# Three gathers of expert rows in flight instead of two

## The reference

```
x = x + attention(layernorm(x))
h = layernorm(x)                                  # 4096 tokens of 128
logits = h @ router_w.T                           # 16 experts
score  = sigmoid(top-1 logit), 0 for the others
routed = sum over experts of down(up * silu(gate)), gate and up from (h * score) @ gate_up_proj[expert]
shared = (silu(h @ shared_gate_w.T) * (h @ shared_up_w.T)) @ shared_down_w.T     # 512 wide
x = x + shared + routed
```

## Time and profile before

| | |
|---|---|
| Median of 3 runs | 231.84 us (228.6 to 233.66) |
| Profiled execution, its own time | 231.57 us |
| Its span, first to last instruction | 229.8 us |
| TensorE, VectorE, ScalarE, GpSimd busy | 88%, 72%, 52%, 53% of the span |
| Mean granted clock of TensorE | 0.946 of full speed |
| The 32 gathers on GpSimd | 32.5 us busy, 33.8 us idle ahead of them |

### The profile page before, as it was taken

The page is one execution under the profiler, slowest core; times in us unless marked ns, Lnnn a source line. Parts: engine busy times, 40 slices in busy tenths (PEclk is TensorE's granted clock), DMA queues, the critical chain, the costliest instruction groups (busy, mean ns, idle before and its releaser), DMA issues.

```text
span 229.8 us, 3715 instructions
## 1 busy us (share of the span) xinstructions
PE 202.2 (88%) x1081; PEld 158.4 (69%) x1081; DVE 165.8 (72%) x437; ACT 119.6 (52%) x237; POOL 122.2 (53%) x143
## 2 busy tenths in 40 slices
PE   7874998889899887689885999999998999999972
PEld 7533754657667866578563889999886877778641
DVE  1599999999999955546677377976435667676773
ACT  2423565566584686732555367554444555636441
POOL 5003336749966866446747666731006675666540
PEclk9998899999999997755999799999999999999999
DMA  4999994120010111111124547533341131322514
GB/s 118 270 333 337 297 228 130 61 93 26 13 35 28 35 47 47 35 51 35 35 59 106 115 106 184 137 84 94 91 130 34 34 91 44 85 79 58 140 34 137
DMA packets 33399, 23.54 MB, mean 102 GB/s; under 512 B 2914, under 2 KB 30564, under 8 KB 33380
## 3 DMA queue, kind: packets, MB, share of 16 engines
q1 hardware_dynamic: 30752, 18.85, 30.9%
q0 software_dynamic: 2048, 4.26, 6.6%
q10 hardware_dynamic: 580, 0.20, 0.4%
HBM read 13.87 MB, written 9.44 MB: 101 GB/s over the span
## 4 chain that ended last, share of the span: by engine, by line
PE 48%; DVE 34%; issue 6%; ACT 3%; DMA 3%; SPq 2%; POOL 1%; ACTq 1%; DVEq 0%
PE quad_banks L1217 8%; DVE qkv L784 7%; PE quad_banks L1218 7%; PE quad_banks L1219 7%; PE bank L1373 4%; DVE ss L802 4%; DVE st L748 4%; PE bank L1276 3%; DVE s_spl L881 3%; DVE rn L810 3%; PE bank L1278 2%; PE bank L1277 2%; DMA w_qkv<-L_attn_Wv 2%; PE bank L1337 2%; DVE ss L806 2%
## 5 line engine op out<-in xcount | busy, mean ns | idle before, releaser
L457 POOL DMA_INDIRECT h_rows<-y_slots,gpos x32 | 32.5, 1015 | 33.8 <-DMA y_slots<-yg 16.7
L390 POOL DMA_INDIRECT x_slots<-h_rows,pos x32 | 31.1, 972 | 16.0 <-issue 8.8
L876 DVE TENSOR_TENSOR s_act<-quad_banks,sg_act 128x512 f32<-128x512 f32 x32 | 22.0, 689 | 20.7 <-ACT sg_act L550 16.2
L550 ACT ACTIVATE sg_act<-quad_banks 128x512 f32<-128x512 f32 x32 | 19.2, 600 | 32.0 <-PE quad_banks L1219 25.3
L362 POOL TENSOR_TENSOR qkv<-qkv,rn 128x512 f32<-128x512 f32 x16 | 16.9, 1078 | 32.5 <-DVE rn L810 32.5
L881 DVE TENSOR_TENSOR s_spl<-s_act,s_spl 128x512 fp32r<-128x512 f32 x32 | 25.7, 809 | 1.7 <-issue 1.7
L1168 PE MATMUL quad_banks<-w_c,xT 128*128 128x384 f32 x64 | 23.5, 492 | 2.2 <-DVE qkv L784 1.4
L556 ACT CAST s_spl<-s_act 128x512 fp32r<-128x512 f32 x32 | 19.6, 614 | 5.6 <-PE bank L1278 4.5
L784 DVE SCALAR_TENSOR_TENSOR qkv<-quad_banks,rs,b_qkv 128x384 f32<-128x384 f32 x32 | 17.8, 602 | 1.8 <-PE quad_banks L1168 1.7
L1276 PE MATMUL bank<-s_spl,sdT 128*128 128x512 f32 x32 | 14.6, 456 | 4.5 <-DVE s_spl L881 4.0
L1168 PEld LDWEIGHTS quad_banks<-w_c,xT 128*128 128x128 f32 x64 | 11.2, 194 | 9.5 <-issue 5.0
(11 more groups left out here) (167 smaller groups left out, 529.4 us busy)
## 6 DMA issues: line engine op xcount, KB each, us to landing
h_rows<-x_slots SPq DMA_DIRECT2D x47, 66.0 KB, 1.9
y_slots<-yg SPq DMA_DIRECT2D x11, 256.0 KB, 2.4
xT<-L_attn_x_turned SPq DMA_DIRECT2D x8, 256.0 KB, 6.5
xres<-L_attn_x SPq DMA_DIRECT2D x8, 256.0 KB, 6.2
w_raw<-L_ffn_gate_up_proj SPq DMA_DIRECT2D x4, 512.0 KB, 5.1
out<-xres SPq DMA_DIRECT2D x8, 256.0 KB
x_slots<-zero_rows SPq DMA_DIRECT2D x1, 1056.0 KB, 14.1
x_slots<-zero_rows SPq DMA_DIRECT2D x1, 990.0 KB, 10.6
```

Of the source, the lines that this page charges most:

```text
L390: g.indirect_dma_start(out=x_slots, out_offset=bass.IndirectOffsetOnAxis(ap=pos[:, t:t + 1], axis=0), in_=h_rows[:, t, :], in_offset=None) ...
L457: g.indirect_dma_start(out=h_rows[:, t, 0:D], out_offset=None, in_=y_slots, in_offset=bass.IndirectOffsetOnAxis(ap=gpos[:, t:t + 1], axis= ...
L876: v.tensor_tensor(s_act[:, k % 2], pair[:, 2 * (k % 2) + 1], sg_act[:, k % 2], ALU.mult).then_inc(s_act_rdy, 1)
```

## The change

The number of gathers in flight becomes a constant, IN_FLIGHT = 3. There are three semaphores instead of two, gather t counts on semaphore t mod 3, and before it is issued GpSimd waits for gather t-3 in place of t-2. In `gathered(c)` VectorE waits on all three, each with the count of those of the first 4(c+1) gathers that fall to it.

```diff
+    IN_FLIGHT = 3
...
-        gath = [sem("gath0"), sem("gath1")]
+        gath = [sem(f"gath{r}") for r in range(IN_FLIGHT)]
...
             for t in range(NT):
-                if t >= 2:
-                    pool.wait_ge(gath[t % 2], 16 * (t // 2))
+                if t >= IN_FLIGHT:
+                    pool.wait_ge(gath[t % IN_FLIGHT], 16 * (t // IN_FLIGHT))
                 g.indirect_dma_start(out=h_rows[:, t, 0:D], out_offset=None, in_=y_slots,
                                      in_offset=bass.IndirectOffsetOnAxis(ap=gpos[:, t:t + 1], axis=0)
-                                     ).then_inc(gath[t % 2], 16)
+                                     ).then_inc(gath[t % IN_FLIGHT], 16)
...
             def gathered(c):
-                for landed in gath:
-                    dve.wait_ge(landed, 16 * (c + 1) * Q // 2)
+                for r, landed in enumerate(gath):
+                    dve.wait_ge(landed, 16 * len(range(r, Q * (c + 1), IN_FLIGHT)))
                 return h_rows[:, Q * c:Q * c + Q, 0:D]
```

## The result

| | before | after |
|---|---|---|
| Median of 4 runs each | 232.75 us (228.6 to 234.28) | 261.2 us (259.35 to 266.34) |
| Profiled execution | 231.57 us | 259.35 us |
| Its span, mean granted clock | 229.8 us, 0.946 | 257.6 us, 0.901 |

The changed kernel was slower: ratio 1.132, 95% interval 1.108 to 1.156. (The ratio is of the fast executions alone, those within 1.5% of the fastest of their kernel, so it is a little above the 1.122 of the two medians.) The forecast was 231.6 us. A second timing of the unaltered changed kernel gave 265.07 us, and a single run at a third time gave 231.72 us. Both numbers belong to the result, and most of what follows is about the difference between them.

What follows compares the result with a forecast made beforehand. The prediction took TensorE's shared-expert work to bound the end, with no gather on the chain. Span 229.8 us, minus 0 plus 0 (up to +0.2), and 1.77 us around it gave 231.6 us; range 228.6 to 233.6 us.

Steps and rivals of the forecast that it cites:

- The waits on GpSimd: GpSimd's gathers: ordinary waits for landings vanish, 31 steps take 40.8 us, GpSimd ends 6 to 10 us sooner; worth 0.
- Who could use the earlier landing: VectorE's sums and the output stores: they stand behind shared-expert products at TensorE's pace, so they don't move: 0.
- three signs of being wrong: End moves over a microsecond with TensorE's last chunk in place; gathers' mean well above 1.02 us; sums with gathered rows idle.
- The cover: Shared expert on TensorE hides the gathers; if it were gone, up to 7.7 us would show.
- The waits on VectorE: VectorE's sums with gathered rows: eight added semaphore waits, 0 to 0.2 us on the path, taken as 0.
- the transfers: DMA queues: gathers form a denser stream, over by about 217, and the last three stores have the queues to themselves: 0.
- The rule weighed: VectorE operations with two SBUF inputs contend with GpSimd reading SBUF; three gathers ran longer, 1.28 to 1.46 us.
- the slow rival: Gathers slowed beside VectorE's splits and sums: 237.0 us, deciding from a step of 1.60 us; chance 0.04.
- Gathers that bind in ordinary executions: Rival: slow landings use up the end's cushion of about 1.1 us, so the change gives 228.6 us; chance 0.13.
- the 0.07 us: Last VectorE sum with gathered rows (L958): the most its start may have been delayed by gather 31's landing.

Runs made afterwards that it cites:

- the bursts: Changed kernel, but three gathers go out in a row, then GpSimd waits for all three to land: 246.79 us, and 243.07 us on another occasion.
- the run of 233.4 us: Changed kernel's three semaphores, but each gather waits for the gather before the last, so two are in flight: 233.4 us, one run without late signals.
- the run of 235.07 us: Kernel before, two gathers in flight, plus 620 increments of an unused semaphore by SyncE: 235.07 us, one run.
- the first set: Runs on one chip without late signals: kernel before 233.28 us, three semaphores with two in flight 231.42 us, four in flight 231.65 us.
- the fifth: Runs on an occasion with late signals at the scatters: kernel before 232.85 us over 7 runs; the changed kernel was not run.
- the true pause: Changed kernel with a GpSimd memset behind each gather, for whose end GpSimd waits: 231.6 and 230.45 us, then 233.29 us over 4 runs.

## Why the prediction was wrong

*The waits on GpSimd.* Right in what GpSimd does: the waits of 13.0 us went to nothing, and the 31 steps took 39.5 us (forecast 40.8). **Wrong in the last sentence of that step**, which priced the earlier end of the gathers at 0, and in the next, *Who could use the earlier landing*, which took the shared expert to go on "at TensorE's pace" and gave no reason why that pace would stay. The step had looked only for who waits for a gather. It did not ask what the gathers' rate does to others that wait for something else. The waits had a use that no view of waits shows: they kept the stream of gathers thin. In the result that was worth 28 us, 25.0 in idle time of TensorE and 5.8 in its clock, less the 3.0 of an earlier start; on the occasion of 231.72 us it was worth nothing. None of the prediction's three signs of being wrong covers this: the end moved, but TensorE's last chunk moved with it.

*The cover.* The step said that the shared expert on TensorE hides the gathers. It does: the last sum never waited for a gather in the changed kernel. But that cover and the thing covered are joined by signals, and the cover was what suffered. That the gathers become the end if the cover is short was shown by the bursts (two waits of 6.3 us).

*The waits on VectorE and the transfers.* Right: 0. Three semaphores with the old order cost nothing that could be seen, and no sum with gathered rows has idle time.

*The rule weighed, and the slow rival made of it.* The contention is real but decides nothing. The step counted three long gathers; the trace of before has five more of 1.03 to 1.19 us, among them the 1.14 at 214.30 of the earlier trace rows, and each of them too began beside a VectorE operation with both inputs in SBUF. In the changed kernel four are longer in the same way (1.08 to 1.18 us), but the mean went down to 0.968 us and the step to 1.27, far from the 1.60 at which that rival decides. It was right that a denser stream could hurt, and looked for the damage in the gathers; its 5.4 us have nothing to do with the 28 measured.

*Gathers that bind in ordinary executions.* Not what happened, but there is something in it. With two in flight and no stall, the last sum was once idle for 2.0 us in the run of 233.4 us, with no releaser named, and in the run of 235.07 us once for 3.6 us, for a gather; so such executions exist, at more than the 0.07 us that the forecast had seen. On the occasion without the stall the changed kernel had 231.72 against 235.29 us, both single runs, so that a gain of the change there (1.5% by these two) is possible and isn't shown.

*What the trace of before could have told.* It had the stall in small, at the scatters, which are also indirect DMAs of GpSimd, and come at the same pace in groups. Timelines of GpSimd, TensorE and ScalarE of the kernel before:

```profile
83.59 0.96 POOL L390 DMA_INDIRECT x_slots<-h_rows,pos  x1 [0.35 <-issue]
84.86 0.96 POOL L390 DMA_INDIRECT x_slots<-h_rows,pos  x1 [0.30 <-DMA x_slots<-h_rows,pos]
```

```profile
84.90 0.66 PE L1157 MATMUL bank<-ident,h_rows 128*128 128x128 f32 x4
```

```profile
86.80 0.59 ACT L509 COPY hT_whole<-bank 128x512 f32<-128x512 f32 x1 [1.69 <-PE bank L1157]
```

Scatters come 1.26 us apart; the transposes end at 85.56, and ScalarE, idle, copies their result at 86.80, 1.2 us later. On the occasion without the stall the same copy is idle for 0.49 us only. During the gathers of the kernel before, at 1.567 us a step, no signal is late. Someone who had set each wait's start against its releaser's end, and not only added up waits, would have had a slow rival with a mechanism, though not its size.

## What stays open

What differs between the occasions isn't known. It isn't one chip against another alone, since the record gives the same chip for the first set and the fifth. All executions here are recorded by the profiler, and on occasions with the stall (the trace of before is one of them, with 305) only 87 to 368 of the 512 increments of the gathers' landings are in the records, against 500 to 512 on those without it. So whether the recording takes part in the stall, or only suffers with it, wasn't tried and can't be told from these runs. Nor is the mechanism settled: the runs show that TensorE's updates are held, that it goes with a dense stream of gathers, and that it ends a few microseconds after the stream. Whether increments without gathers can bring it is open, and so is the direct comparison of the change with its pause on one occasion. It isn't the fetching of instructions: no packet of those queues falls between 183 and 228 us. No version was shown to beat both kernels: the one with the true pause took 233.29 us against 232.85, and the difference is inside the spread of either.

## What to carry to other kernels

Taking away a wait of GpSimd that was on nobody's path cost 28 us here on two occasions and nothing on a third. A wait that nobody waits for may still be doing work, as a brake on what is sent out; before taking it away, ask what the rate does to the others' signals as well as who needs the result. To look for it, set the end of each signalling instruction beside the start of the idle engine that waits for it, paired by their count and not by what stands nearest, in stretches of the old trace where the same kind of stream already runs at the pace that the change will bring. And time a surprising result on more than one occasion: the same kernel was 12 to 13% slower twice and no slower once.

## What the runs showed of the hardware that wasn't expected

- TensorE's semaphore updates, as a rule 0.01 us behind their instructions, came up to 22.5 us late (matmul ended at 192.77, update at 215.30) beside gathers with a step of 1.25 us, on some occasions only; at 1.44 to 1.5 us none was late.
- Those of VectorE and ScalarE that are recorded were on time in the same stretch. The Trainium skill, "SBUF — State Buffer", section "Who interferes with whom", says of TensorE and ScalarE that they never wait on anyone, which is about ports. Here ScalarE stood idle for 6.5, 11.5 and 15.0 us, most of it with its input ready, and its wait was for a signal.
- A memset of 0.17 us on GpSimd behind a gather fits nearly whole into the 0.30 us before the next: the step went only from 1.25 to 1.28 us. With a memset of 0.22 us and a wait of GpSimd for its end, the step was 1.44 us.
